# Two fields instead of three in the record of an edge sort: what it does to a graph layer on one core

## The reference

```python
xn = _layernorm(x, axis=-1)
# _L0_gnn_ref(xn, src, dst, edge_weight, W, b): edge_row = src, edge_col = dst
msgs = edge_val[:, None] * x[edge_col]
agg = jax.ops.segment_sum(msgs, edge_row, num_segments=N_NODES)
return jnp.einsum('nf,of->no', agg, W) + b
```

## Time and profile before

| | |
|---|---|
| median of 3 runs | 1410.53 us (1410.11 to 1412.51) |
| the profiled execution | 1414.44 us, span of its instructions 1411.9 us |
| mean granted TensorE clock | 0.924 |
| TensorE busy (matmul) | 1160.9 us, 82% |
| VectorE busy | 860.1 us, 61% |
| GpSimd busy | 614.4 us, 44% |
| ScalarE busy | 536.1 us, 38% |
| the main loop | from about 183 to about 880 us |

### The profile page before, as it was taken

One profiled execution on the slowest core, in us unless ns is written; L12 is line 12 of the kernel. 1 busy time (PEld: TensorE's weight loads), 2 busy tenths in 40 slices (PEclk: granted clock), 3 DMA queues, 4 the chain that ended last, 5 costly groups with the idle time before them and its releaser, 6 DMA issues.

```text
span 1411.9 us, 21461 instructions
## 1 busy us (share of the span) xinstructions
PE 1160.9 (82%) x6731; PEld 1004.4 (71%) x6731; DVE 860.1 (61%) x1960; ACT 536.1 (38%) x1247; POOL 614.4 (44%) x584
## 2 busy tenths in 40 slices
PE   0679945989989989899899898872399999999990
PEld 0457634877868868778778786672399999999980
DVE  1963135888888898888988985876522222222225
ACT  0344542764855746647557464121111111111100
POOL 1530175465665764755756656100433333333320
PEclk9879977999999999999999999965599999999995
DMA  3301132222222222222222223020589999999958
GB/s 107 96 24 34 45 100 74 64 82 71 80 77 71 83 73 66 88 70 76 77 73 79 75 70 92 16 89 3 200 290 332 336 329 332 333 333 328 332 185 272
DMA packets 118265, 196.10 MB, mean 139 GB/s; under 512 B 13420, under 2 KB 67498, under 8 KB 118186
## 3 DMA queue, kind: packets, MB, share of 16 engines
q1 hardware_dynamic: 92074, 123.82, 26.4%
q0 software_dynamic: 26112, 71.34, 16.0%
HBM read 177.12 MB, written 17.99 MB: 138 GB/s over the span
## 4 chain that ended last, share of the span: by engine, by line
PE 53%; DVE 21%; DVEq 9%; issue 8%; ACT 3%; DMA 2%; SPq 2%; another core or an unknown queue 2%; ACTq 0%; POOL 0%; POOLq 0%
PE psum L941 16%; PE psum L951 8%; PE psum L874 5%; DVE agg L1173 5%; PE psum L864 5%; PE psum L672 4%; PE psum L703 2%; PE psum L805 2%; DVE agg L1179 2%; ACT in_slot L382 2%; PE psum L755 2%; PE psum L712 1%; DVEq L1032 1%; DVE record L1057 1%
## 5 line engine op out<-in xcount | busy, mean ns | idle before, releaser
L609 POOL DMA_INDIRECT arena<-y_rows,gather_i x416 | 445.2, 1070 | 352.6 <-PE psum L864 115.0
L864 PE MATMUL psum<-arena,hot 128*128 128x256 f32 x832 | 227.9, 404 | 18.5 <-issue 7.5
L1173 DVE TENSOR_TENSOR agg<-psum,agg 128x256 f32 x416 | 174.4, 419 | 79.1 <-issue 21.2
L466 ACT ACTIVATE arena<-arena,listed 128x256 f32<-128x256 f32 x416 | 175.1, 495 | 73.8 <-DMA arena<-y_rows,gather_i 73.8
L864 PEld LDWEIGHTS psum<-arena,hot 128*128 128x128 f32 x832 | 154.4, 199 | 57.7 <-issue 25.5
L941 PEld LDWEIGHTS psum<-arena 128*128 128x128 f32 x1536 | 180.6, 194 | 6.2 <-issue 4.2
L941 PE MATMUL psum<-arena 128*128 128x128 f32 x1536 | 182.2, 278 | 2.0 <-DVE arena L1491 2.0
L1498 DVE TENSOR_TENSOR arena<-psum,arena 128x512 f32<-128x512 f32 x64 | 44.3, 692 | 215.1 <-PE psum L941 212.1
L550 ACT ACTIVATE arena<-psum 128x512 f32<-128x512 f32 x64 | 38.2, 597 | 335.5 <-issue 202.5
L632 POOL DMA_INDIRECT chosen_rows<-arena,back_at x64 | 63.2, 987 | 220.6 <-DVE arena L1505 215.9
L382 ACT ACTIVATE in_slot<-iota,place_f 128x128 f32<-128x128 f32 x416 | 127.0, 388 | 77.5 <-DVE place_f L1036 67.1
(11 more groups left out here) (208 smaller groups left out, 1588.0 us busy)
## 6 DMA issues: line engine op xcount, KB each, us to landing
arena<-in_L_ffn_w_dram SPq DMA_DIRECT2D x144, 512.0 KB
xnT<-in_L_ffn_w_dram SPq DMA_DIRECT2D x48, 512.0 KB
arena<-y_rows,gather_i POOLq DMA_INDIRECT x416
arena<-chosen_rows SPq DMA_DIRECT2D x8, 640.0 KB, 8.9
agg<-in_x_dram SPq DMA_DIRECT2D x4, 640.0 KB, 10.3
y_rows<-arena SPq DMA_DIRECT2D x4, 640.0 KB, 3.6
n_rows<-arena SPq DMA_DIRECT2D x4, 640.0 KB
out_dram<-agg SPq DMA_DIRECT2D x4, 640.0 KB
```

The lines of the kernel that those rows point to most:

```text
L466: last = act.activation(rows[h][:, t, :], rows[h][:, t, :], ACT.Copy, scale=weight[h][:, t:t + 1])
L609: pool.indirect_dma_start(rows[h][:, t, :], None, y_rows, bass.IndirectOffsetOnAxis(ap=gather_i[h][:, t:t + 1], axis=0)).then_inc(gathered ...
L864: pe.matmul(bank_of(g, t // 2)[:, (t % 2) * C:(t % 2 + 1) * C], hot[:, n % HOTS, :], rows[h][:, t, :], start=True, stop=True).then_inc(met, 1)
L1173: dve.tensor_tensor(own, bank_of(g, t // 2)[:, (t % 2) * C:(t % 2 + 1) * C], own, ALU.add).then_inc(evicted, 1)
```

## The change

`src` and `dst` are folded into one number, `dst * 4096 + src`, which is below 2 to the 24th. The record has two fields, the folded number and the weight, and the matmul moves 64 columns. When the list is read, the folded number is copied out as int32; a shift by 12 gives the gather's index, a mask with 4095 the node, which is copied into float32. In the loop, the instructions of steps 24, 30, 39 and 48 are gone. At the start, two casts become one multiply-add.

```diff
-    FIELDS = 3
+    FIELDS = 2
+    FOLD = 4096
...
+        folded = sb("folded", [P, 2, GT], I32)
...
             def read_list(g):
                 h = g % 2
                 dve.wait_ge(reordered, (g + 1) * CHUNKS)
                 dve.drain()
-                dve.tensor_copy(gather_i[h][:, :], in_order[:, GT:2 * GT])
-                dve.tensor_copy(listed[h][:, :, :], in_order.rearrange("p (f t) -> p f t", f=FIELDS)[:, 0:3:2, :])
+                dve.tensor_copy(folded[:, 0, :], in_order[:, 0:GT])
+                dve.tensor_copy(weight[h], in_order[:, GT:2 * GT])
                 dve.tensor_copy(bin_of[h][:, :], bins_of_tiles[0:1, :])
                 dve.tensor_copy(start_i[:, 0, :], ends_row[:, 0:CROSS])
 
             def place_list(g):
                 h = g % 2
+                dve.drain()
+                dve.tensor_scalar(gather_i[h][:, :], folded[:, 0, :], 12, None, ALU.arith_shift_right)
+                dve.tensor_scalar(folded[:, 1, :], folded[:, 0, :], FOLD - 1, None, ALU.bitwise_and)
+                dve.drain()
+                dve.tensor_copy(node[h], folded[:, 1, :])
                 dve.drain()
                 dve.scalar_tensor_tensor(node_in_bin[h][:, :], bins_of_tiles, -float(P), node[h], ALU.mult, ALU.add)\
                     .then_inc(list_kept, 1)
...
             dve.wait_ge(edges_loaded, 96)
-            dve.tensor_copy(edge[:, 0, :], edge_i[:, 0, :])
-            dve.tensor_copy(edge[:, 1, :], edge_i[:, 1, :])
+            dve.scalar_tensor_tensor(edge[:, 0, :], edge_i[:, 1, :], float(FOLD), edge_i[:, 0, :], ALU.mult, ALU.add)
             dve.drain()
...
-                for k, at_steps in enumerate(((23, 24, 27), (29, 30, 32), (36, 39, 43), (46, 48, 49))):
+                for k, at_steps in enumerate(((23, 27), (29, 32), (36, 43), (46, 49))):
                     if step in at_steps:
                         make_field(g, k, at_steps.index(step))
```

More of the change, by code:

```diff
@@ L59, in gps_layer @@
     assert NG == (NT + 1) // 2 and NT == U * TURNS and GE * NG == COLS and 0 < LAST_ROW <= COLS and ETILES % WS == 0
+    assert N <= FOLD and FOLD * FOLD <= 2 ** 24
     assert GE % CH == 0 and GT % GC == 0 and CROSS % 2 == 0 and CROSS <= 32 and GT % BATCH == 0 and CROSS % BATCH == 0
@@ L274, in _ @@
             sp.wait_ge(edges_padded, 1)
-            for a, b in ((edge_i[:, 0, :], src), (edge_i[:, 1, :], dst), (edge[:, 2, :], edge_weight)):
+            for a, b in ((edge_i[:, 0, :], src), (edge_i[:, 1, :], dst), (edge[:, 1, :], edge_weight)):
                 sp.dma_start(a[0:P - 1, :], b[0:(P - 1) * COLS].rearrange("(p c) -> p c", c=COLS)).then_inc(edges_loaded, 16)
@@ L555, in _ @@
             pool.memset(edge_i[96:P, :, LAST_ROW:COLS], 0)
-            pool.memset(edge[96:P, 2, LAST_ROW:COLS], 0.0)
+            pool.memset(edge[96:P, 1, LAST_ROW:COLS], 0.0)
             pool.drain().then_inc(edges_padded, 1)
```

## The result

The changed kernel is slower: 1419.97 us (1415.48 to 1423.24, 8 runs) against 1411.26 (1409.37 to 1414.66, 8 runs), a ratio of 1.0057 with a 95% interval of 1.0043 to 1.0072. I had forecast 1411.1, no change, and a range that ended at 1415.5. The profiled execution took 1417.2 us with a span of 1414.5. Of all executions on record one, of the kernel before, took 1787.96 us at a mean granted clock of 0.647 where all others have 0.917 to 0.934, and it is in none of the ratios.

A forecast was written before the change was run, and what follows sets the result against it. VectorE was taken to bound the start and the loop from 595.5 to the next `place_f`, TensorE other stretches. Start -1.4 and turns +2.0 gave +0.6 us: median 1411.1, range 1402.5 to 1415.5.

The forecast's parts named there:

- start, to the first gather: Edges' landing to first gather: four fields off VectorE's chain and cheaper casts, 1.44 us shorter; bounds nothing to 2.2.
- fields, 11 turns: Four record instructions gone from VectorE in each sorting turn: -0.41 us a turn, bounds -0.34 and -0.68.
- list, 11 turns: Unfolding in `place_list` ahead of `node_in_bin` on VectorE: +0.59 us a turn, bounds +0.43 and +0.73.
- falls of the clock in the loop: TensorE's clock dropping behind its 2.63 us gap: pattern within one of today's 5 in 11 turns, 0.45.
- Steps 24 and 30: Fields between `place_f` and VectorE's 1.65 us wait for TensorE: removing them gains nothing.
- step 39: Field just before an eviction that needs step 41's matmul: removing it gains 0.07 us a turn.
- Step 48: Field on VectorE's leading stretch, 605.24 to 605.58: removing it gives all of its 0.34 us a turn.
- The matmuls: Reorder on TensorE: 64 columns instead of 96 gain zero; bounds zero and 0.6 us for each reorder on the chain.
- The rival with shorter ones: Reorder matmuls shrink with their columns, 10.2 us in all: 1401.5 us, chance 0.06.
- two falls more: TensorE's clock falls behind more loop gaps: +3.2 us, 1414.3; chance of more falls 0.18.
- fewer: TensorE's clock falls behind fewer loop gaps: three less is -4.8 us, 1406; none, 1403; chance 0.22.

The follow-up runs named there:

- first comparison: Changed kernel against the kernel before, 8 runs each: 1419.97 us against 1411.26, ratio 1.0057.
- second: Changed kernel, run again unchanged, against the kernel before: 1420.47 us, ratio 1.0072.
- filled kernels: Five matmuls added in TensorE's gap: kernel before 0.9953, changed kernel 0.9971, kernel before with only the list's work 1.0007, changed kernel without unfolding 0.9938.
- plane2: Changed kernel with three edge planes kept in SBUF and the weights in the third, as before: ratio 1.0057 to the kernel before.
- two_ops: Changed kernel with a cheaper unfolding, one multiply-add and one drain added instead of three instructions and two drains: ratio 0.9994 to the kernel before.
- after_again: Changed kernel run again, unchanged: 1420.47 us, ratio 1.0072 to the kernel before.
- before_again: Kernel before run again, unchanged: ratio 1.0000.
- before_look: One more profile of the unchanged kernel before: six falls, first gather at 172.06; no ratio given.
- after_look: One more profile of the unchanged changed kernel: seven falls, first gather at 174.73; no ratio given.
- fields_only: Changed kernel without the unfolding, `dst` in place of the folded number: ratio 0.9979 to the kernel before.
- swapped ones: ScalarE's first-half `hidden_relu` moved ahead of `slot_hot`: kernel before 0.9854, changed kernel 0.9880, changed kernel with a cheaper unfolding 0.9901.

## Why the prediction was wrong

The forecast was +0.6 us; measured are +8 (first comparison) and +10 (second). By the three profiles of each kernel and the turns of the filled kernels the parts are:

| term | forecast | measured |
|---|---|---|
| start, to the first gather | -1.4 | +1.5 |
| fields, 11 turns | -4.5 | -3.2 |
| list, 11 turns | +6.5 | +6.6 |
| falls of the clock in the loop | 0 | +2.3 |
| sum | +0.6 | +7.2 |

**The start, the step that failed most.** I took it as VectorE's time carried through unchanged, 1.44 us of it. The fields did come off: from `in_tile` of chunk 0 to TensorE's third reorder it is 30.5 us in every profile with three fields and 29.2 in every one with two, 1.34 us less. But `in_tile` itself starts later. I had written that GpSimd's long sums "start from VectorE's own `xn`, so they move along". The first ones don't: they follow an addition of two bias rows, which waits for the landing of a DMA. Timelines of GpSimd and VectorE in the kernel before:

```profile
44.38 0.73 POOL L591 TENSOR_TENSOR bias_row<-bias_row 128x256 f32<-128x256 f32 x1 [38.98 <-DMA bias_row<-in_L_gnn_b_dram]
```

```profile
46.79 5.33 DVE L999 TENSOR_SCALAR arena<-agg,x_stat,x_root 128x256 f32<-128x256 f32 x5
52.21 3.15 DVE L1049 TENSOR_TENSOR in_tile<-place_i,iota 128x256 f32<-128x256 int32 x1
```

VectorE's five instructions of line 999 take 1.71 us elsewhere and 5.33 here, because they stand still while GpSimd's second sum runs (48.10 to 51.00). In the changed kernel the same two points are:

```profile
45.14 0.73 POOL L594 TENSOR_TENSOR bias_row<-bias_row 128x256 f32<-128x256 f32 x1 [39.74 <-DMA bias_row<-in_L_gnn_b_dram]
```

```profile
52.96 3.16 DVE L1052 TENSOR_TENSOR in_tile<-place_i,iota 128x256 f32<-128x256 int32 x1
```

In all 18 profiles `in_tile` starts 7.82 to 7.87 us behind the addition of the bias rows, wherever VectorE took up the edges. So the later start on the edges costs nothing and the multiply-add gains nothing; what counts is that the biases come 0.96 us later on the mean of the three profiles (45.14, 45.46 and 45.59 against 44.38, 44.49 and 44.45). plane2, with its early edges, has them at 45.04, and two_ops, with late edges, at 44.57 and the takeover at 81.58. Why they land later stays open. TensorE takes over at 82.13, 82.46 and 82.58 instead of 82.72, 82.84 and 82.78, 0.4 us earlier and not 1.44. Then the clock takes that and more. The first gather starts at 171.02, 173.87 and 174.73 against 171.86, 171.31 and 172.06, so 1.9 us are lost behind the takeover: -1.34 + 0.96 + 1.86 = +1.5. In windows of after_again (us, busy of PE, PEld, DVE, ACT, POOL, granted clock, DMA), and then of before_again, TensorE is at its lower level once more around 109:

```profile
109.00:111.00 2.00, 2.00 (x8) 1.72 (x8) 1.93 (x3) 1.16 (x3) 0.00 (x0) 0.50 0.00 0
```

```profile
109.00:111.00 2.00, 2.00 (x14) 1.82 (x13) 1.75 (x5) 0.25 (x1) 0.00 (x0) 1.00 0.00 0
```

The slow ten transposes at 107 stand in 7 of the 8 profiles with a fold (all but the first), in none of the 8 with three fields, and in neither of the 2 with two fields and no unfolding. From TensorE's takeover to the first gather it is 90.7 to 92.2 us in those 7 and 88.5 to 89.3 in the other 11. I had seen the low clock at 84 and bounded the start with it, at nothing to -2.2; a later fall was not in the bound, and why the unfolding goes with it is not shown.

**The list: right.** +0.59 forecast, +0.60 measured, and nothing absorbed it.

**The fields: right in place, small in size.** Steps 24 and 30 gave nothing and step 39 gave 0.08, as worked out. Step 48 gave 0.29 and not 0.34: I had let the eviction start 0.57 us behind `add_dense`, as the field did, and it starts 0.62 behind. Of these 0.37 us, 0.29 arrived at `bin_of`, instead of 0.41.

**The matmuls: right.** 112 ns from record to record at 64 columns as at 96. The rival with shorter ones should have read 1400.9 us instead of 1401.5, as its sum counts the 0.6 twice; nothing else used it.

**The falls: the wrong likeliest case.** I had "two falls more" as the rival on the slower side at 0.18, 1414.3 us, and my reason against it was that a fall makes the next gap safe. That held at every gap in the one profile I had (in before_look it failed once, at the first two gaps), and it failed in the changed kernel, where two fell in a row at 414.83 and again at 697.70:

```profile
414.83 3.52 PE L758 MATMUL psum<-xnT,wq 128*128 128x256 f32 x8 [2.63 <-ACT relu_h L462]
...
471.99 2.67 PE L758 MATMUL psum<-xnT,wq 128*128 128x256 f32 x8 [2.62 <-ACT relu_h L462]
```

The kernel before showed 5, 5 and 6 falls, the changed one 6, 7 and 7. A fall adds 1.69 us between query and the eviction of step 39 (12.08 instead of 10.39), so 1.33 more are 2.3 us. That I forecast a longer turn and still gave more falls less chance than fewer (0.18 against 0.22) was the error: each of the kernels with longer turns had more.

**What stays open.** The parts sum to 7.2 us, within the interval of the first comparison (6.1 to 10.2 us) and just under that of the second (7.8 to 12.5). They leave out the loop's last turn and all that follows it. The spans of the profiles, the three of the changed kernel against the two of the kernel before that took as long as the first comparison's (1411.9 and 1412.3), differ by 5.3 us: the last turn is shorter by 3.2 (51.2 on the mean against 54.5) and the rest longer by 2.1 (550.6 against 548.6). Whether either belongs to the change is not shown. Filling the gap saved 13 us in the changed kernel and 6.6 in the other, more than 1.33 falls explain; the intervals of these ratios, 1.4 to 2.4 us to each side, cover only part of it.

## What to carry to other kernels

Count a removed instruction only on the stretch where its engine leads: here four instructions of 0.34 us in a turn bought 0.29, and three short ones with two drains on that stretch cost 0.60. If TensorE has a gap in every turn that its clock sometimes falls behind, price the change for more falls, not only for the same number, and look first at the gap itself: moving one call in another engine's order was worth 20 us, more than anything in the change. And ask of every wait at the start which landing it hangs on: 0.96 us of a late bias row took most of the 1.34 us that four instructions gave.

## What the runs showed of the hardware that I had not expected

A gap of 2.63 us on TensorE, once in every turn of 55 to 59 us, is followed by its lower clock in 4 to 8 of 11 cases; each fall costs 1.5 to 1.7 us. The loop's first gap is shorter in some profiles: at 1.93 to 2.12 us it was followed by a fall in all four (before_look, after_again, after_look, fields_only), at 1.27 or 1.28 us in none of three. From the loop's second turn on, no fall followed the gaps of 0.47 to 0.89 us of the filled kernels or those of up to 1.76 us of the swapped ones. A float32 matmul with a new 128x128 weight runs at 112 ns from record to record for 64, 96 and 128 columns alike. On VectorE, shift, mask, drain, copy and drain on 128x32 elements took 0.60 us, where one multiplication of 128x256 took 0.34 from start to start: for such lists the number of dependent steps is the price, not the elements. While a sum of 128x1280 on GpSimd runs, VectorE's layernorm instructions stand still: 5.33 us instead of 1.71. And the same kernel took 15 us less in some groups of runs than in others, of which 11 to 13 lie between the first gather and the loop's first gap (75.4 us in one profile, 62.7 in the other). Two groups with the same chip number on record differ by this much, so what makes it is open.
